# Moving the masked product of an attention step behind its output projection and side unit, and the W1 sums ahead of the output squares

## What is computed

```python
xn  = layernorm(x)                                   # x: 2048 x 1024 per core
q, k = (xn @ Wq.T), (xn @ Wk.T)                      # 16 heads x 16 features
v   = xn @ Wv.T                                      # 16 heads x 64
qf, kf = taylor_exp(q), taylor_exp(k)                # [1, q/2, q (x) q / (4 sqrt 2)], 273 features
y   = tril(qf @ kf.T) @ v
y   = y * rsqrt(mean(y * y) + 1e-5) * g              # per head
attn = y @ Wo.T
h   = gelu(xn @ ternary(W1).T + b1)                  # 4096 hidden
ffn = h @ ternary(W2).T + b2                         # ternary: threshold 0.5 * mean(|W|)
out = x + attn + ffn
```

## Time and profile before

| | us |
|---|---|
| median of 3 runs (slowest core) | 760.08 (760.06 to 760.13) |
| time of the profiled execution | 760.95 |
| its span, first to last instruction, slowest core | 759.2 |
| spans of the 8 cores | 753.8 to 759.2 |
| TensorE busy | 691.8 (91%) |
| VectorE (DVE) busy | 417.8 (55%) |
| ScalarE (ACT) busy | 243.4 (32%) |
| GpSimd (POOL) busy | 99.1 (13%) |

### The profile page before, as it was taken

The page is one execution under the profiler, slowest core; times in us unless marked ns, Lnnn a source line. Parts: engine busy times, 40 slices in busy tenths (PEclk is TensorE's granted clock), DMA queues, the critical chain, the costliest instruction groups (busy, mean ns, idle before and its releaser), DMA issues.

```text
span 759.2 us, 11498 instructions; the slowest of 8 cores (753.8 to 759.2 us)
## 1 busy us (share of the span) xinstructions
PE 691.8 (91%) x4050; PEld 335.8 (44%) x4050; DVE 417.8 (55%) x623; ACT 243.4 (32%) x322; POOL 99.1 (13%) x131
## 2 busy tenths in 40 slices
PE   2777888877789888999999999999999999999998
PEld 1344544544445444444444444444444444444443
DVE  6667564678577566276556435351554554401653
ACT  3456666657557443222333333333100000000000
POOL 3112222224122211000000001010010000000000
PEclk9999999999999999999999999999999999999999
DMA  7974464766848624659786614533353676200883
GB/s 155 204 161 103 87 122 92 171 146 194 216 143 261 201 69 128 171 198 303 216 281 175 213 56 131 200 114 110 111 200 133 206 223 195 98 1 20 244 232 115
DMA packets 65415, 121.49 MB, mean 160 GB/s; under 512 B 22096, under 2 KB 28112, under 8 KB 65360
## 3 DMA queue, kind: packets, MB, share of 16 engines
q1 hardware_dynamic: 46752, 64.46, 28.0%
q0 software_dynamic: 18608, 56.30, 27.2%
HBM read 103.30 MB, written 16.78 MB: 158 GB/s over the span
## 4 chain that ended last, share of the span: by engine, by line
PE 81%; ACT 6%; DMA 5%; issue 4%; DVE 2%; POOL 2%; SPq 0%; ACTq 0%; DVEq 0%; POOLq 0%
PE pST L1199 8%; PE pY L1221 7%; PE pSS L1199 7%; PE pST L1221 7%; PE pW L1199 7%; PE pW L1221 7%; PE pSS L1221 7%; PE pY L1199 7%; PE pSS L977 4%; PE pW L1134 4%; PE pW L977 4%; PE pSS L1134 3%; ACT Am L922 3%; DMA xr<-x 2%; PE pSS L966 2%
## 5 line engine op out<-in xcount | busy, mean ns | idle before, releaser
L1221 PE MATMUL pY<-w2t,hT 128*128 128x512 bf16 x256 | 66.0, 379 | 0.1
L1221 PE MATMUL pST<-w2t,hT 128*128 128x512 bf16 x256 | 66.0, 379 | 0.0
L1221 PE MATMUL pSS<-w2t,hT 128*128 128x512 bf16 x256 | 66.0, 379 | 0.0
L1221 PE MATMUL pW<-w2t,hT 128*128 128x512 bf16 x256 | 66.0, 379 | 0.0
L524 POOL TENSOR_SCALAR_AFFINE_SELECT Am<-Am 128x1024 bf16<-128x1024 bf16 x32 | 35.3, 1104 | 208.4 <-ACT Am L922 208.4
L1199 PE MATMUL pST<-xnT,w1t 128*128 128x512 bf16 x272 | 61.5, 379 | 0.0
L1199 PE MATMUL pSS<-xnT,w1t 128*128 128x512 bf16 x256 | 57.9, 379 | 0.4 <-DVE consts L705 0.4
L1199 PE MATMUL pW<-xnT,w1t 128*128 128x512 bf16 x256 | 57.9, 379 | 0.0
L1199 PE MATMUL pY<-xnT,w1t 128*128 128x512 bf16 x240 | 54.2, 379 | 0.0
L719 DVE TENSOR_SCALAR w1t<-stg,consts 128x2048 bf16<-128x2048 f32 (+1 forms) x18 | 21.0, 1165 | 54.1 <-PE pY L1199 53.9
L517 POOL DMA_DIRECT2D stg<-w1r x32 | 25.1, 784 | 163.3 <-DVE w1t L722 147.5
(11 more groups left out here) (185 smaller groups left out, 1043.0 us busy)
## 6 DMA issues: line engine op xcount, KB each, us to landing
stg<-w1r POOLq DMA_DIRECT2D x32, 1024.0 KB, 7.5
stg<-w2r SPq DMA_DIRECT2D x16, 1024.0 KB, 9.0
stg<-w2r POOLq DMA_DIRECT2D x16, 1024.0 KB, 7.1
xr<-x SPq DMA_DIRECT2D x16, 512.0 KB, 5.2
res_scr<-rst SPq DMA_DIRECT2D x16, 512.0 KB, 3.2
res<-res_scr SPq DMA_DIRECT2D x32, 256.0 KB, 3.6
xs<-x SPq DMA_DIRECT2D x32, 256.0 KB, 3.9
out<-osb SPq DMA_DIRECT2D x32, 256.0 KB, 2.5
```

The lines of the kernel that those rows point to most:

```text
L1221: return e.matmul(out_bank(n), hT[:, j, 128 * t:128 * t + 128], w2t[8 * dh + j // 4][:, j % 4, :], start=(j == 0), stop=(j == NJ - 1))
```

## The change

`y_within(i)` is issued behind `proj_out(i - 3)` and `side(...)`, except in step 2. ACT's order follows: the W1 sum and the copy of the side unit come in front of the output square. DVE's order becomes W1 sum, copy of the projection, copy of `qk`, square sum (step 2: square sum first).

```diff
+SIDE_LATE = 2
 # DVE
+        def square_sums(i):
+            b = i % 2
+            e.wait_ge(aYS, i + 1)
+            e.tensor_reduce(cc(C_SS + 8 * b, 8),
+                            ysq[:].rearrange("p (h f) -> p h f", h=8, f=E),
+                            AX, ALU.add).then_inc(dRD, 1)
...
-            e.wait_ge(aYS, i + 1)
-            e.tensor_reduce(cc(C_SS + 8 * b, 8),
-                            ysq[:].rearrange("p (h f) -> p h f", h=8, f=E),
-                            AX, ALU.add).then_inc(dRD, 1)
+            if i == SIDE_LATE:
+                square_sums(i)
+            if i in A1_SLOT and A1_SLOT.index(i) in A1_DVE:
+                n = A1_SLOT.index(i)
+                abs_sum(("a1", n), C_A1 + n)
             if i >= 19:
                 empty_wo(i - 3)
             if side_unit(i) is not None and side_unit(i)[0] == "qk":
                 empty_qk(B + 1)
-            if i in A1_SLOT and A1_SLOT.index(i) in A1_DVE:
-                n = A1_SLOT.index(i)
-                abs_sum(("a1", n), C_A1 + n)
+            if i != SIDE_LATE:
+                square_sums(i)
 # ACT
-            e.wait_ge(pYD, i + 1)
-            e.activation(ysq[:], pY[:, 512 * b:512 * b + 512],
-                         AF.Square).then_inc(aYS, 1)
             if i in A1_SLOT and A1_SLOT.index(i) in A1_ACT:
                 n = A1_SLOT.index(i)
                 abs_sum(("a1", n), C_A1 + n, sA1)
             if side_unit(i) is not None and side_unit(i)[0] != "qk":
                 empty_side(side_unit(i))
+            e.wait_ge(pYD, i + 1)
+            e.activation(ysq[:], pY[:, 512 * b:512 * b + 512],
+                         AF.Square).then_inc(aYS, 1)
 # TensorE
-            y_within(i)
+            if i == SIDE_LATE:
+                y_within(i)
             if i >= 19:
                 proj_out(i - 3)
             if side_unit(i) is not None:
                 side(side_unit(i))
+            if i != SIDE_LATE:
+                y_within(i)
```

## The result

The changed kernel takes 765.11 us (median of 4 runs, 764.13 to 767.83) against 760.11 us (760.06 to 760.93): a ratio of 1.0070 with a 95% interval of 1.0054 to 1.0087. It is slower by some 5 us, beyond the upper end of the forecast range (763.5). The profiled execution took 767.83 us, with a span of 766.2 on its slowest core.

What follows compares the result with a forecast made beforehand. TensorE bounds from 302 us (busy 453.38 of 456.00); before it, attention-stage waits, with the masked product's as target. Terms summed to +0.3 us on core 5, about +1.7 on core 0; +0.7 was taken: 760.8 us, range 757.0 to 763.5.

Steps and rivals of the forecast that it cites:

- steps 3 to 14: Early attention steps: ACT's moved square and TensorE's moved product make the stage later, +2.1 us in sum at step 14.
- step 15: Attention stage: the side unit loses its 1.75 us wait for the mask, which gives back 0.35 us.
- steps 16 to 19, up to scores(20): W1 sum ahead of DVE's square sum makes ACT wait for the root: +2.75 us on a core like core 0.
- steps 20 to 30: Late attention steps: -0.2 us from the load wait and -1.2 us from the new orders.
- step 31: Last attention step: the projection goes ahead of the product that waited 2.06 us for its mask, -1.4 us.
- the 0.48 a square: ACT's output square between side unit's copy and next `Am` costs +0.48 us each in steps 4, 6, 7 and 8.
- step 3: Attention stage: the squares that `y_before(4)` needs leave ACT one square earlier, -0.5 us.
- steps 20 to 26: Projections no longer wait for the mask but for ACT's copy: -1.2 us in sum against step 19.
- rival 3: Slower by the clock: half-clock stretches behind the two new root waits, 1.65 us each, about 762.9 us; chance 0.20.
- rival 4: Slower, nothing absorbed: step 19's W1 load comes in time, step 18's 4.5 us stay but for 1.2 and 1.4, 762.2; chance 0.12.
- rival 1: Faster by the clock: idle of 3.26 and 1.75 us shrinks, two stretches stay at 2.4 GHz, 757.1 us; chance 0.20.
- rival 2: Faster by ACT: the output square misses the chain of steps 4 to 8, -1.6 us, 758.5 us; chance 0.08.

Runs made afterwards that it cites:

- e10: Changed kernel plus zero-weight products on TensorE in steps 17 and 19 (12 and 10) and 8 more in step 7: ratio 1.0024 to the kernel before.
- e3: Kernel before with the whole new order in steps 15 and 31 alone: 757.31 us against 760.73, ratio 0.9949.
- e9: Changed kernel plus zero-weight products on TensorE in the root waits, 12 in step 17 and 10 in step 19: ratio 1.0033 to the kernel before.
- e6: Kernel before with only ACT's output square moved behind the side unit's copy in steps 4, 6, 7 and 8: ratio 1.0040.
- e5: Kernel before with the new order in steps 3, 15 and 20 to 31 only: 756.13 us against 760.79, ratio 0.9950.
- e11: Changed kernel measured once more with nothing changed: one run, 765.67 us.
- e4: Kernel before with the new order only in steps 0, 1 and 3 to 15: ratio 1.0033.

## Why the prediction was wrong

**The waits.** Cores without a stretch in the piece give each term of the sum without the clock:

| term | forecast | measured | from |
|---|---|---|---|
| steps 3 to 14 | +2.1 | +2.90 | 101.48 (e10) - 98.58 (e3) |
| step 15 | -0.35 | -0.93 | 12.64 - 13.57 (one core of before) |
| steps 16 to 19, up to scores(20) | 4.5 - 1.75 = +2.75 | +3.39 | 27.34 (five cores of e9; +3.6 with the sixth) - 23.95 |
| steps 20 to 30 | -0.2 (load wait), -1.2 (orders) | -1.02 | 94.35 - 95.37 |
| step 31 | -1.4 | -1.74 | 5.38 - 7.12 |
| sum | +1.7 | +2.60 | |

In the first row the 0.48 a square was right: TensorE's wait in step 8 grew by it, and e6 loses 2.35 + 1.0, of which 1.5 is the stretch at 98, so 1.85 for four squares. Wrong is step 3: forecast -0.5, measured +0.4 up to scores(14) (e5), as DVE's late square sum holds up the layernorm. With one early stretch on both sides, e10 core 2 against the core 4 of before, the row would read 102.00 - 99.96 = +2.04, but that nearness is luck: the old stretch had cost 1.37 there. Of the -1.02, -0.63 is the load wait of step 19, so that only -0.39 is left for the gain of steps 20 to 26, a third of the forecast. So step 3 has the wrong sign, the late gain is too large, the other mechanisms were right, and errors of both signs partly cancel.

**The step that failed** is "The forecast leaves core 5 with as many; core 0 would lose the one at 294.7": the number of half-clock stretches. Up to the first `up` core 5 went from 3 to 4 (a fifth lies at 650 us), core 3 from 3 to 5, all cores together from 22 to 30, and to 740 us from 22 to 32. The forecast had 0 for core 5 and -1.65 for an ordinary core; measured are 4.01 - 2.60 = +1.41 of the mean shift. It is 0.69 up to scores(14), where the stretch at 98 us (on two cores at 73) costs more than the one near 65 did, and 30.07 - 27.34 = 2.73 in steps 17 and 19, less 2.0 for what vanished: 1.03 in step 31 (8.8 against 7.12 on five cores), 0.71 in 20 to 31 and 0.27 in 14 to 16. The 0.71 is not all clock: cores 1 and 5 of before had a load wait of 2.48 and 3.26 us on TensorE there with a stretch behind it.

The forecast had this as rival 3 with a chance of 0.20, and as its own condition for being wrong ("changes by more than one"). It priced the two at the new root waits at 1.65 each (measured 1.78 for one and 2.5 more for a second). It did not see the one at step 7, since it looked at single waits of 2 us and more, while there two of 0.81 and 1.32 sufficed. The kernel before already had stretches behind such pairs. On core 5 the one at 66.0 stands behind these:

```profile
64.65 0.59 PE L1062 MATMUL pSS<-qblk,qkT 128*128 128x512 bf16 x2 [1.39 <-ACT qf L878]
...
66.17 0.58 PE L1086 MATMUL pY<-st,qf 128*128 128x256 bf16 x2 [0.72 <-ACT qf L891]
```

**A second error was to follow one core.** For core 5 itself the forecast of +0.3 was near: from scores(3) to the first `up` it took 247.2 where it took 245.3, +1.96, with one stretch more. The 1.6 that the load wait was to absorb came as 1.9. But the single terms (+3.71, -1.43, +5.15, -3.73, -1.74) are again far off and cancel. And a time that is the slowest of eight cores is not core 5's: it was core 4 in the profiled run (stretches up to `up` 2 before, 4 now, and the tail) and core 6 in e11 (5 stretches). Stretches are not all of it: core 1 of before has 4, more than core 5, and ends 2.6 sooner, as its scores(3) came 3.5 sooner. With hindsight, an ordinary core's sum plus two stretches (1.7 + 2 x 1.65 = 5.0) gives 765, but that sum was itself 0.9 too low. The base under rivals 3 and 4 is not that of rival 1 either (760.5 and 760.3 against 760.4), which changes no verdict.

**What held.** `Am(9)` starts 61.09 us behind scores(3) on core 4 and 57.67 on core 5 of before: 3.4 later, 1.5 of it the stretch at 98, which leaves 1.9 for some 1.8 forecast (with the same luck as above), with ACT's order copy, square, `Am`. The root waits were 2.1 to 3.5 us in step 17 and 2.8 in step 19, for some 2 forecast, behind the W1 sum. The waits of 1.75 and 2.06 for the mask are gone. The product itself costs nearly nothing: e6 without it and e4 with it differ by 0.24 in the stage to scores(8). Rival 1 falls with the count of stretches, rival 2 with e6 (the square is on the chain), and rival 4 with the 1.9 us absorbed on core 5.

By the Trainium skill, "TensorE: Matmul & The Clock Gate" ("HAM oscillation"), a long enough wait between groups of matmuls makes the next group start at the throttled clock, each time anew, and it advises to arrange the work so that TensorE stays warm. The trace agrees in the main: 5.30 us for sixteen matmuls behind the waits on core 3, 3.61 with the waits filled. The same page of the Trainium skill (Part 1) says that the monitor's window runs freely, so that the number of slow matmuls varies from run to run; here core 3 has the stretch behind the wait of step 17, and core 4 has not.

## What to carry to other kernels

Do a forecast of an order twice: once for the waits, and once for what each new idle spot of TensorE does to the clock, short ones that lie close together included; a wait of 2.6 us in front of a product cost 4.3 where the stretch fell behind it. Before an instruction is moved on an in-order engine, ask for each step what stands directly behind its new place. A square of 0.6 us on ACT's chain, a layernorm behind a late square sum, and a sum of 2.28 us in front of the one that a root waits for: the pieces with these (3 to 14 and 16 to 20) lost 9.7 us with their stretches, more than the 5.7 that the others gave back. An order that is good in some steps (15, 20 to 31) and bad in others should be chosen step by step. And read a change on eight cores from the means of all cores and from cores with equal stretches, not from the slowest alone.

## What was not expected of the hardware

Adding 22 products to TensorE's stream made the stage from scores(16) to scores(20) shorter by 2.1 us (e9), and 30 took the count of half-clock stretches from 32 to 11 (e10). A stretch costs what the place makes of it: 1.37 us near 65 us on core 4 in the old order, 0.1 (0.5 by scores(14)) at the same place in the new one, 1.78 for the first in steps 16 to 19 (29.12 against 27.34) and 2.5 more for the second (31.66).
